# A GNN kernel's local pass: two of ten layers in full words, and the building of sum matrices on another engine

## The reference, cut to what matters

```python
def _gcn_conv(x, W, b, src, dst, dinv):
    h = x @ W
    norm = dinv[src] * dinv[dst]
    agg = jax.ops.segment_sum(h[src] * norm[:, None], dst, num_segments=x.shape[0])
    agg = agg + (dinv * dinv)[:, None] * h
    return agg + b
...
x = _gcn_conv(node_embedding, W1, b1, src, dst, dinv)     # 128 -> 256
x = _l2norm(x)
def f(z):
    z1 = _gcn_conv(z, Wf1, bf1, src, dst, dinv)           # 256 -> 256
    z1 = _l2norm(z1)
    return _gcn_conv(z1, Wf2, bf2, src, dst, dinv) + z    # 256 -> 256
k1 = f(x)
k2 = f(x + 0.5 * k1)
k3 = f(x + 0.5 * k2)
k4 = f(x + k3)
x = x + (k1 + 2.0 * k2 + 2.0 * k3 + k4) / 6.0
return _gcn_conv(x, W2, b2, src, dst, dinv)               # 256 -> 128
```

## Time and profile before

| | us |
|---|---|
| median of three runs | 7417.72 |
| lowest and highest of them | 7416.8, 7420.82 |
| the profiled execution, whole | 7411.88 |
| its span from first to last instruction | 7408.9 |
| DVE busy in the span | 6278.8 (85%) |
| PE busy in the span | 6235.8 (84%) |
| POOL busy in the span | 4124.5 (56%) |
| ACT busy in the span | 3963.8 (54%) |

### The profile page before, as it was taken

How to read it: one execution, slowest core, us unless ns; L and a number is a source line. 1 busy time by engine, 2 the same in 40 slices (tenths; PEclk the granted TensorE clock), 3 DMA queues, 4 the chain that set the end, 5 groups by cost and what they waited for, 6 DMA issues and landing times. The chain is left out here.

```text
span 7408.9 us, 157945 instructions
## 1 busy us (share of the span) xinstructions
PE 6235.8 (84%) x37260; PEld 5136.6 (69%) x37260; DVE 6278.8 (85%) x16996; ACT 3963.8 (54%) x11296; POOL 4124.5 (56%) x4269
## 2 busy tenths in 40 slices
PE   7698998888999657989989998999888766987776
PEld 3688888888888535867776677667756554865664
DVE  8788888888888777879878987998799887878887
ACT  6566777777777576733671157115722233764443
POOL 0454444447600476855776677667744465646665
PEclk8799999999999898999999999999999998989998
DMA  0465555554444466879779977997799865543432
GB/s 2 118 167 161 158 161 160 162 161 154 144 145 140 149 188 196 247 253 301 230 225 319 336 235 225 326 336 232 226 372 388 283 186 157 170 145 121 125 124 83
DMA packets 981282, 1483.86 MB, mean 200 GB/s; under 512 B 156967, under 2 KB 450705, under 8 KB 980647
## 3 DMA queue, kind: packets, MB, share of 16 engines
q1 hardware_dynamic: 685479, 922.39, 37.4%
q0 software_dynamic: 141504, 309.42, 16.3%
q10 hardware_dynamic: 153664, 244.12, 9.1%
HBM read 902.58 MB, written 573.11 MB: 199 GB/s over the span
## 5 line engine op out<-in xcount | busy, mean ns | idle before, releaser
L1346 PE MATMUL bank<-c_rows,sums_all 128*128 128x256 f32 (+1 forms) x3920 | 1321.7, 420 | 534.9 <-DVE c_rows L1497 377.3
L751 PE MATMUL bank<-wf_w,c_xt 128*128 128x256 f32 x6272 | 1614.5, 380 | 1.9 <-DVE y L1555 1.9
L1391 ACT ACTIVATE c_xt<-bank 128x512 f32<-128x512 f32 (+1 forms) x980 | 556.2, 568 | 1579.4 <-PE bank L1357 1575.5
L1346 PEld LDWEIGHTS bank<-c_rows,sums_all 128*128 128x128 f32 x3920 | 634.5, 194 | 966.5 <-DVE c_rows L1497 787.3
L1317 POOL DMA_INDIRECT c_rows<-t_tab,src_pair x784 | 869.1, 1109 | 709.0 <-PE bank L1346 552.3
L751 PEld LDWEIGHTS bank<-wf_w,c_xt 128*128 128x128 f32 x6272 | 1133.4, 191 | 126.9 <-ACT c_xt L1391 3.4
L1497 DVE SCALAR_TENSOR_TENSOR c_rows<-bank,carry,c_rows 32x256 f32<-32x256 f32 (+1 forms) x1950 | 913.9, 469 | 265.7 <-PE bank L1346 166.1
L1317 POOL DMA_INDIRECT c_rows<-z_tab,src_pair x784 | 764.8, 975 | 288.8 <-issue 186.9
L741 PE MATMUL bank<-wf_hi,lx_hi 128*128 128x256 f32 x3200 | 713.4, 305 | 98.8 <-ACT lx_hi L1017 59.6
L1017 ACT ACTIVATE lx_hi<-bank 128x512 fp32r<-128x512 f32 (+1 forms) x1000 | 574.1, 574 | 392.2 <-PE bank L986 385.6
L1511 DVE SCALAR_TENSOR_TENSOR c_u<-bank,lead,c_own 128x256 f32<-128x256 f32 x1764 | 758.5, 467 | 0.5
(11 more groups left out here) (334 smaller groups left out, 14447.0 us busy)
## 6 DMA issues: line engine op xcount, KB each, us to landing
c_z<-z_tab SPq DMA_DIRECT2D x882, 256.0 KB
z_tab<-lz SPq DMA_DIRECT2D x400, 256.0 KB, 3.1
t_tab<-lt SPq DMA_DIRECT2D x400, 256.0 KB
z_tab<-y ACTq DMA_DIRECT2D x392, 256.0 KB
c_own<-z_tab SPq DMA_DIRECT2D x392, 256.0 KB
t_tab<-y ACTq DMA_DIRECT2D x392, 256.0 KB
c_own<-t_tab SPq DMA_DIRECT2D x392, 256.0 KB
fl_x<-x_tab SPq DMA_DIRECT2D x396, 128.0 KB
```

Source lines behind the costliest of these rows:

```text
L751: last = nc.tensor.matmul(out, x(k), w[:, k, :], start=(k == 0), stop=(k == ks - 1 and not bias))
L1346: nc.tensor.matmul(psum[s % 2][:, i * win:(i + 1) * win], sums[:, j * 2 + i, :], rows[:, s, i, 0:win], start=True, stop=True).then_inc(S[" ...
L1391: nc.scalar.activation(xt[:, s % 2].rearrange("p k n -> p (k n)")[:, 0:n], psum[2 + s % 2][:, 0:n], ACT.Copy).then_inc(S["copied"], 1)
```

## The change

Three things, all in the local pass:

1. Layers 0 and 9 ("first" and "last") are multiplied in full fp32 words. ACT copies the transposed rows as they are into buffers of their own (`x_first`, `x_last`, two each), DVE's `low` falls away for these slots, and PE makes one product (`full_product`) in place of three. PE's next transpose into that bank waits for `high` in place of `low`.
2. The split weights of these two layers are no longer made ahead of the pass.
3. `build` goes from DVE to POOL, with a lag of 12 slots in place of 0, and its instructions are written out there.

```diff
-        for name, ks, width in (("w1", 1, H2), ("wf1", 2, H2), ("wf2", 2, H2), ("w2", 2, D)):
+        for name, ks, width in (("wf1", 2, H2), ("wf2", 2, H2)):
             early(name + "_hi", [P, ks, width], F32R)
             early(name + "_lo", [P, ks, width], F32R)
...
+        parted = [1 if kind[layer[q]] in ("mid", "end") else 0 for q in range(Q)]
...
+        def full_rows(b, q):
+            return (x_first if layer[q] == 0 else x_last)[:, q // 2 % 2]
...
+                def build(b, q, odd):
+                    n, k = divmod(q, 10)
+                    if k not in (0, 2, 4):
+                        return
...
+                    if k == 0:
+                        pool.wait_ge(S[f"s_rows{s}"], b * 32 + 16 * (n // 2 + 1))
+                        nc.gpsimd.tensor_copy(rows_f[:, s, :], rows_i[:, s, :]).then_inc(S["s_built"], 1)
+                        return
...
+                    ins = nc.gpsimd.tensor_scalar(built[:, s, i, :], rows_f[:, s, i * P:(i + 1) * P],
+                                          m["dst_f"][:, bass.ds(b * 8 + (n * 2 + i), 1)], None, ALU.is_equal)
...
-                staggered(pool, blocks, Q, early, [(0, gather_x), (12, make_tables)], unrolled=True)
+                staggered(pool, blocks, Q, early, [(0, gather_x), (12, make_tables), (12, build)], unrolled=True)
...
-                    if prev:
+                    if prev and parted[prev[1]]:
                         pe.wait_ge(S["low"], ph.at("low", *prev))
+                    elif prev:
+                        pe.wait_ge(S["high"], ph.at("high", *prev))
...
-                    pe.wait_ge(S["low"], ph.at("low", b, q))
+                    if parted[q]:
+                        pe.wait_ge(S["low"], ph.at("low", b, q))
...
+                        if not parted[q]:
+                            last = full_product(nc, psum[4 + n][:, i * width:(i + 1) * width],
+                                                lambda k: full_rows(b, q)[:, k, i * P:(i + 1) * P],
+                                                m[w + "_w"], ks)
+                            continue
...
                 def low(b, q, odd):
-                    n = H2 if layer[q] == 0 else 2 * H2
+                    if not parted[q]:
+                        return
+                    n = 2 * H2
...
                 staggered(dve, blocks, Q, early,
-                          [(6, normalise), (1, low), (3, add_rest), (3, take), (5, invert), (0, build)])
+                          [(6, normalise), (1, low), (3, add_rest), (3, take), (5, invert)])
```

More of the change, by code:

```diff
@@ L705, in _ @@
                 act.wait_ge(S["weights_in"], 64)
-                for n, (name, ks, width, _) in enumerate(parts):
+                for n, (name, ks, width, _) in enumerate(parts[2:]):
                     last = nc.scalar.activation(m[name + "_hi"][:, 0:ks, :], m[name + "_w"][:], ACT.Copy)
@@ L788, in local_pass @@
         x_lo = sb("lx_lo", [P, 4, 2, H2], F32R)
+        x_first = sb("lx_first", [P, 2, 1, H2])
+        x_last = sb("lx_last", [P, 2, 2, H2])
         squares = sb("lsquares", [P, 4, 2, H2])
@@ L817, in local_pass @@
         rooted = [1 if kind[layer[q]] != "end" else 0 for q in range(Q)]
+        parted = [1 if kind[layer[q]] in ("mid", "end") else 0 for q in range(Q)]
         one = [1] * Q
         rates = {
-            "turned": one, "high": one, "low": one, "product": one, "taken": one,
+            "turned": one, "high": one, "low": parted, "product": one, "taken": one,
             "rest_set": [[0, 0, 0, 0, 1, 0, 1, 0, 3, 1][layer[q]] for q in range(Q)],
@@ L896, in make_tables @@
                         next(tables, None)
+                def build(b, q, odd):
+                    n, k = divmod(q, 10)
+                    if k not in (0, 2, 4):
+                        return
+                    if isinstance(b, int) and 4 * b + n >= builds:
+                        return
+                    s = n % 2
+                    if k == 0:
+                        pool.wait_ge(S[f"s_rows{s}"], b * 32 + 16 * (n // 2 + 1))
+                        nc.gpsimd.tensor_copy(rows_f[:, s, :], rows_i[:, s, :]).then_inc(S["s_built"], 1)
+                        return
+                    if k == 2:
+                        pool.wait_ge(S["s_built"], b * 8 + 2 * n + 1)
+                        if not isinstance(b, int) or 4 * b + n >= 2:
+                            pool.wait_ge(S[f"s_out{s}"], b * 32 + 16 * (n // 2))
+                    i = k // 2 - 1
+                    ins = nc.gpsimd.tensor_scalar(built[:, s, i, :], rows_f[:, s, i * P:(i + 1) * P],
+                                          m["dst_f"][:, bass.ds(b * 8 + (n * 2 + i), 1)], None, ALU.is_equal)
+                    if k == 4:
+                        ins.then_inc(S["s_built"], 1)
                 nc.gpsimd.memset(eps[:], LN_EPS).then_inc(S["constants_set"], 1)
-                staggered(pool, blocks, Q, early, [(0, gather_x), (12, make_tables)], unrolled=True)
+                staggered(pool, blocks, Q, early, [(0, gather_x), (12, make_tables), (12, build)], unrolled=True)
                 for _ in tables:
@@ L1013, in high @@
                     act.wait_ge(S["turned"], ph.at("turned", b, q))
-                    prev = ph.back(b, q, 4)
+                    alone = isinstance(b, int) and b in (0, blocks) and not parted[q]
+                    prev = ph.back(b, q, 2 if alone else 4)
                     if prev:
                         act.wait_ge(S["product"], ph.at("product", *prev))
-                    nc.scalar.activation(x_hi[:, k].rearrange("p k n -> p (k n)")[:, 0:n], psum[k][:, 0:n],
-                                         ACT.Copy).then_inc(S["high"], 1)
+                    nc.scalar.activation((x_hi[:, k] if parted[q] else full_rows(b, q)).rearrange("p k n -> p (k n)")[:, 0:n],
+                                         psum[k][:, 0:n], ACT.Copy).then_inc(S["high"], 1)
                 def begin_rest(b, q, odd):
@@ L1148, in take @@
                                         ).then_inc(S["taken"], 1)
[L1150 to L1169, removed]
                 def invert(b, q, odd):
```

3 lines of the change are left out of this document (1 added, 2 removed).

## The result

The changed kernel takes 7320.16 us (median of four runs, 7314.69 to 7322.69) against 7417.68 for the kernel before in the same session: ratio 0.9867, 95% interval 0.985 to 0.9884, 97.5 us less. The forecast was 7325. The profiled execution took 7322.69 us with a span of 7320.9.

A forecast was written before the change was run, and what follows sets the result against it. DVE was taken to bound the first 39.7 us of each 87.2 us block, ACT and PE the rest. 7411.9 - 103 (DVE work removed) + 10 (sharing with POOL) = 7319, 7325 on the median's footing; range 7302 to 7375, at 0.80.

The forecast's parts named there:

- The frame: Local pass: 25 blocks of 87.2 us, each three stretches with different bounds; a DVE saving counts fully only in the first.
- the first stretch: Layer pairs 3/8 and 4/9 of a block, 39.7 us, DVE busy 36.8; to become 35.6 and stay DVE's.
- the other two: Rest of a block: 20.7 us bound by ACT (pair 0/5), 26.8 us bound by PE (1/6, 2/7); savings there counted nothing.
- The terms: DVE's first stretch, per block: 2.40 us for layer 9, 0.66 for layer 0, 1.05 for builds; 103 us in 25 blocks.
- Every second block: Jump of the two-block loop, said to come in every second block: DVE stands 4.67 us with no releaser, carried over unchanged.
- The sharing of DVE and POOL: First stretch: POOL's builds delay DVE by half their time in a third of it, 10 us (0 to 58); whole-length rival 0.05.
- the prediction's 21 us: Sharing cost by the skill page's rule that DVE waits for POOL's whole instruction: 21 us, not 10, forecast 7336.
- POOL's price: Builds on POOL: 1.4 us each (1.0 to 3.8), 136 us for 98 builds, 370 at the upper end.
- The cover: POOL's own waiting before L669, 563.5 us, 35 us a block over the first sixteen blocks, hides the builds.
- PE's product of the last layer: Layer 9's products on PE: 0.61 us each against 1.38, leaving PE 29.3 us of work in the first stretch.
- The clock: Rival: PE's granted clock stays down through pair 4/9, blocks 3 us longer, 7451 us; chance 0.05.
- SP waited for POOL: Rival: late builds hold SP's stores and DVE's take; from 4.1 us a block it eats the gain; chance 0.03.

The follow-up runs named there:

- PE's old length put back: Changed kernel with the first half of the last layer's product computed twice, so PE works as long as before: 7327.57 us.
- tried in layers 3 and 8: Two kernels: changed kernel with one layer's lx_lo cut to 2 columns, PE's split product kept: 7301.6 us for layer 3, 7288.32 for layer 8.
- the doses: Changed kernel with POOL's cast and comparisons cut to 2 columns, 7323.31 us, or with each comparison done twice, 7333.09 us, set beside the changed kernel.
- the 2-column builds: Changed kernel with the cast and both comparisons of each build on POOL cut to 2 columns: 7323.31 us.

## Why the prediction was right, point by point

**The frame held.** The bound of the first stretch was DVE's and still is, the other two kept their lengths, and DVE idles 2.8 us in the first where it idled 2.9. With PE's old length put back, the quiet stretch did not grow. In the first and last layer the waits for `lx_lo` fall away together with DVE's work, and no run parts these two; that the work alone counts was tried in layers 3 and 8.

**The terms.** Full words were put at 76 us, and alone they gave 83: the stretch gave a little less than counted, the rest of a block and the jump a little. The builds were put at 26 us with 10 off for the sharing, so 16; alone they gave 20, and on top of the full words 15. The forecast's 93 became 97.5. That it came out within 5 us is in part luck: the stretch gave less than counted, and gains that were put at nothing, of the rest of a block and of the gaps beside the builds, made up for it. "Every second block" with a jump was an error without effect: the loop makes ten rounds of two blocks and jumps back nine times, and the other blocks are written out.

**The sharing of DVE and POOL** was put at 10 us, and the runs show some 8 to 11, by DVE's lengths and by the doses. The size of its cause was off in both directions: POOL's arithmetic is 180.9 us and not 136, and DVE loses less of it than the half that I took from the earlier trace rows. With a stretch of 36 of 83.2 us and a third of it open to the delay, half of 180.9 would be 13 us. The whole-instruction rule of the Trainium skill, page "SBUF — State Buffer", section "SBUF: two separate sides", would by the same sum make it 26 us if DVE came second every time; the measured 8 to 11 lie nearer to the half. POOL's lengths above show that POOL waits too, so the prediction's 21 us, with DVE as the only loser, was not the rule's whole reading. That the two errors, POOL's time too low and DVE's share too high, left the term at its size was luck.

**POOL's price** was mis-sized, without effect. By columns I had put a comparison at 0.35 us (its own bounds 0.17 to 0.52) and the cast at 0.69; they take 0.69 and 0.47. The rows chosen misled: L582 took 522 ns for 396 columns, less than a comparison of 128, and L571's cast of 396 took 1067. POOL's timeline before has rows that are nearer in columns, and without any scaling they give 0.36 + 2 x 0.73 = 1.82 us a build, where 1.85 was measured:

```profile
130.79 0.73 POOL L565 TENSOR_SCALAR key<-fill_rank 128x196 f32<-128x196 f32 x1 [123.96 <-DVE fill_rank L484]
134.21 0.36 POOL L569 CAST own_key<-key 128x196 int32<-128x196 f32 x1
```

Scaling by columns is wrong besides, since an operation of 2 columns takes half of the full one's time. The 3.8 us at the upper end still held it. The cover was there: POOL's waits absorbed it. It was smaller than the 563.5 us counted, since in 169.9 of them POOL waited for nothing that the profile shows, and not for SP's stores (393.6).

**PE's product of the last layer** was put at 0.61 us from the earlier trace rows. It steps by 0.90 (PE's timeline after):

```profile
1299.57 1.06 PE L750 MATMUL bank<-w_w,lx_last 128*128 128x128 f32 x8
1300.47 0.60 PE L1014 MATMUL bank<-ident,lt 128*128 128x128 f32 x4
```

The x4 there against x8 here shows why: the row of the coupled stage was the product of one tile, and a slot of the local pass holds two (its four matmuls stand as eight records in the trace). PE's saving is 0.48 us a product in place of 0.77, and PE's work in the stretch is 31.39 us in place of 29.3. None of it counted.

**The other rivals.** The clock did not fall more often: PE's granted clock over the pass is 0.99 where it was 0.97. Nor is the gain the clock's: over the nine quiet stretches it is 0.99 before and 1.00 after, and 1.00 both times in the block shown. SP waited for POOL 3.2 us in all. The sums of three operands grew from 690 to 699 ns over the pass and to 706 in the block shown, less than the tenth that I allowed.

## What to carry to other kernels

Cut the program where its bound changes and price a saving only in the stretch of the engine that it frees; here PE's saving was worth nothing and DVE's nearly its whole time. That price holds only until the next engine is full: PE idled 4.5 us in the stretch, and with layers 4 and 8 added 1.1 were left. Count, too, which operations start inside the stretch: of layers 3 and 8 two of four did not. When a duration is taken from another stage, check that the row covers the same amount of work, by its count, and look through all rows of the operation before scaling one.

## What the hardware showed that I had not expected

A comparison with a per-partition number on POOL takes 351 ns for 2 columns and 691 for 128, a cast 234 ns for 2 and 466 for 256 (means, with the waits for DVE in them). DVE needs 333 and 288 ns for the full ones, so the larger surprise is how little the shorter ones save.

DVE's stall where the two-block loop jumps is not a constant of the kernel: the stretches with a jump are longer than the quiet ones by 3.8 us before, 3.7 in the changed kernel, 3.3 with full words alone, 4.6 with the 2-column builds and 5.2 with layer 8 in full words, at the same length of loop or nearly so. Against the kernel before, that is 5 us less to 13 us more over the nine jumps, as large as the smaller terms tested here, and no row names a releaser for it. What sets it stays open. Differences of some 10 us between single kernels are therefore better read from the quiet blocks than from the whole time.
